# Gated attention with squares on ScalarE and inverse roots by tile, and a causal output projection of rounded parts

## The chip, the cores and the metric

The kernel runs on one core of a Trainium2 chip, as one launch. The metric is the device time in microseconds (us). A core has TensorE (PE, products; PEld is its loading of weights), VectorE (DVE), ScalarE (ACT), GpSimd (POOL) and SyncE (SP, which here issues every DMA). They run their own streams of instructions and meet at semaphores.

## The reference, cut to what matters

x has 16 tiles of 128 tokens with 256 features. Six layers are added to it in turn. Two are touched:

```
# layer 0: causal attention, 16 heads of 64
q, k, v = (layernorm(x) @ w_q, @ w_k, @ w_v)          # 256 -> 1024 each
out = softmax(causal(q k^T / 64)) v                   # per head
x = x + out @ w_u + b_u                               # 1024 -> 256

# layer 3: gated attention, 16 heads of 16
Q, K, V = (xn @ Wq.T + bq, ...)                       # 256 -> 256 each
Qn, Kn = Q / max(|Q|, 1e-12), K / max(|K|, 1e-12)     # per head
heads = softmax(Qn Kn^T / 4) V
heads = heads * sigmoid(g) * sigmoid(mean_tokens(gelu(xn @ Wg1.T + bg1) @ Wg2.T + bg2))
x = x + heads @ Wo.T + bo
```

All tensors are float32.

## The kernel before

Every layer is a stage with tensors and semaphores of its own, and a barrier between stages. A stage handles x in eight pairs of tiles (`PAIRS`); a pair i has tiles b = 0 and 1. Each engine's program is written out by hand inside a loop over the pairs (`pairs_by_two`: three turns of two pairs in a hardware loop, then two written out); work for later pairs stands between that for pair i. Nothing reorders it: what an engine does next is the order of its lines. `Chain.link` makes an engine wait for its own last instruction.

"Rounded parts": a float32 operand is split into a high part in TensorE's rounded format (fp32r) and a low part (what is left), and `split_product` makes one product out of three (high x high, high x low, low x high).

The causal stage (`stage_causal_attention`, `CausalAttention`; tensors a_...). `produce` makes slots of a ring of two banks with rounded parts of xn and of the weights (`w`, from `w_nat`, whose low parts VectorE makes in `weight_low`, one for each of q, k, v). A pair has eight units u of four heads: `pe_scores`, `dve_max`, `act_exp`, `dve_normalise` (probabilities times the inverse of their sum), `pe_transpose`, `copy_probT`, `pe_weighted`. Every second unit VectorE copies a chunk of 512 columns out of `out_bank` into `attnT` (`copy_out`, chunks 0 to 3; chunk 3 after the last unit). Then `pe_project` multiplies attnT with w_u, 8 products for each tile, in float32 without splitting, and `dve_residual` adds the result to x. GpSimd adds the bias b_u to x (`add_bias`) and takes the root for the layernorm (`ln.root`).

The gated stage (`stage_gated_attention`; also a_...). A ring of two banks turns through these slots; those named for a later pair are made that far ahead: xn (of i+2, transposed), hidden (i+1, the gate's), qk0 and qk1 (i+2, queries and keys of tile 0 and 1, 512 columns), logits (i+1), turn_q and turn_k (i+1, transposes of the scaled queries and keys), values (i+1). A slot waits until the slot two before it has been emptied. Beside them stand `scores(i, b)`, `weigh(i, b)` (probabilities times values, and times ones for the sums, into `out[b]`) and `project(i, b)`, into the same bank. VectorE: `empty` of qk adds the bias; `sum_squares` squares queries and keys of both tiles, sums per head and bounds the sum; GpSimd's `invert` raises the 64 sums to -1/2; `scale_heads` multiplies both tiles with it; `normalise` takes the reciprocal of the probabilities' sums and multiplies; `add_residual` adds to x. ScalarE empties xn, hidden (gelu), logits and turn_q and does the `exponentials`.

## Time and profile before

| | |
|---|---|
| runs, median of 3 | 2009.88 us (2009.46 to 2011.67) |
| profiled execution, its own time | 2011.48 us |
| its span in the profile | 2009.8 us |
| TensorE busy | 1842.6 us, 92% |
| VectorE busy | 1327.1 us, 66% |
| ScalarE busy | 649.5 us, 32% |
| GpSimd busy | 175.8 us, 9% |
| TensorE's granted clock, mean | 0.964 |

The span is what the profiled execution shows from its first to its last instruction; its own time has 1.7 us around it. Busy shares are over the whole span. In the profile's rows a tile keeps the name of its stage's prefix (a_ for both attention stages here; the causal one lies before 375 us, the gated one between 1143 and 1346 us). An instruction that waited shows in brackets how long its engine had been idle and who released it. [...]

### The profile page before, as it was taken

To read this page: it belongs to the slowest core of one execution; us is meant where nothing else is said; L and a number is where in the kernel's file an instruction comes from. 1 tells how busy PE (TensorE), PEld (TensorE's weight loads), DVE (VectorE), ACT (ScalarE), POOL (GpSimd) and SP (SyncE) were. 2 spreads that over 40 slices of the span, in tenths; PEclk is the share of its full clock that TensorE was granted. 3 is DMA by queue.
4 is the path that set the end of the run, shared out by engine and by line. 5 is a ranking of instruction groups with operands and counts; after the bars stand their busy time and mean duration, and the time that the engine had idled before them with its cause. 6 is when DMAs were issued, how large, how long until landed. Compare 5 with 4: busy or idle time off the path is not lost. (4 is left out here: it accounts for less than half of the span.)

```text
span 2009.8 us, 43767 instructions
## 1 busy us (share of the span) xinstructions
PE 1842.6 (92%) x16819; PEld 1541.4 (77%) x16819; DVE 1327.1 (66%) x3598; ACT 649.5 (32%) x1504; POOL 175.8 (9%) x125
## 2 busy tenths in 40 slices
PE   6999999699749999999999878878899999999998
PEld 5887787477638888888888645557788888888887
DVE  4555555377668988888988446646666666666664
ACT  3444434244342211221122035426333333323332
POOL 0000000011000000000000046531000000000000
PEclk9999999799879999999999879979899999999999
DMA  4000000222060000000000130001212010111101
GB/s 159 1 1 0 0 0 1 48 64 63 1 131 8 8 7 3 7 7 8 3 7 1 35 85 1 0 1 38 33 16 32 16 31 16 29 18 27 20 0 43
DMA packets 139319, 48.61 MB, mean 24 GB/s; under 512 B 108178, under 2 KB 138418, under 8 KB 139186
## 3 DMA queue, kind: packets, MB, share of 16 engines
q1 hardware_dynamic: 139186, 46.66, 10.4%
q8 instruction: 105, 1.72, 0.4%
q14 instruction: 28, 0.23, 0.0%
HBM read 42.43 MB, written 4.19 MB: 23 GB/s over the span
## 5 line engine op out<-in xcount | busy, mean ns | idle before, releaser
L2849 DVE TENSOR_TENSOR m_act_up<-m_silu,m_up 128x512 f32<-128x512 f32 x136 | 93.5, 687 | 168.0 <-PE m_up L587 125.0
L2768 ACT ACTIVATE m_silu<-m_gate 128x512 f32<-128x512 f32 x136 | 81.5, 599 | 379.6 <-PE m_gate L587 379.6
L2833 DVE SCALAR_TENSOR_TENSOR g_x<-m_y,m_combine,g_x 128x256 f32<-128x256 f32 x272 | 118.8, 479 | 52.8 <-PE m_y L587 51.3
L233 ACT ACTIVATE a_prob<-a_score,a_neg_max 128x128 f32<-128x128 f32 x256 | 90.7, 367 | 170.3 <-DVE a_neg_max L223 170.3
L2404 PE MATMUL f_out<-f_ko,f_gel 128*128 128x256 f32 x512 | 123.9, 394 | 2.4 <-issue 1.3
L2447 ACT ACTIVATE f_gel<-f_act 128x512 f32<-128x512 f32 x128 | 76.6, 598 | 131.7 <-PE f_act L587 90.9
L2404 PE MATMUL f_turn<-f_ko,f_gel 128*128 128x256 f32 x512 | 111.8, 379 | 0.0
L2404 PEld LDWEIGHTS f_out<-f_ko,f_gel 128*128 128x128 f32 x512 | 96.1, 194 | 17.1 <-issue 4.1
L587 PE MATMUL f_act<-f_hT_pair_high,f_kiT_high 128*128 128x256 f32 x384 | 108.2, 282 | 0.0
L2404 PEld LDWEIGHTS f_turn<-f_ko,f_gel 128*128 128x128 f32 x512 | 97.3, 190 | 13.2
L587 PE MATMUL f_act<-f_hT_pair_high,f_kiT_low 128*128 128x256 f32 x384 | 107.3, 279 | 0.0
L587 PE MATMUL f_act<-f_hT_pair_low,f_kiT_high 128*128 128x256 f32 x384 | 107.3, 279 | 0.0
L2839 DVE TENSOR_TENSOR m_hidden_low<-m_act_up,m_hidden_high 128x512 fp32r<-128x512 f32 x136 | 93.2, 685 | 1.5
L1281 POOL TENSOR_TENSOR a_inv<-a_ss,a_inv_power 128x64 f32<-128x64 f32 x8 | 84.6, 10571 | 71.7 <-DVE a_ss L1485 71.7
L2762 ACT CAST m_hidden_high<-m_act_up 128x512 fp32r<-128x512 f32 x136 | 83.4, 613 | 18.9 <-DVE m_act_up L2849 18.9
L587 PE MATMUL m_y<-g_wT_high,m_hidden_high 128*128 128x256 f32 x288 | 81.9, 284 | 2.9 <-DVE g_x L2833 1.9
L587 PE MATMUL m_y<-g_wT_high,m_hidden_low 128*128 128x256 f32 x288 | 81.8, 284 | 0.0
L587 PE MATMUL m_y<-g_wT_low,m_hidden_high 128*128 128x256 f32 x288 | 81.5, 283 | 0.0
L587 PE MATMUL a_ring<-a_xnT_high,a_w_high 128*128 128x256 f32 x256 | 77.1, 301 | 4.5 <-DVE a_w_low L544 4.4
L2437 ACT ACTIVATE g_shared<-g_shared 128x64 f32<-128x64 f32 x16 | 4.1, 256 | 235.8 <-DVE g_shared L2483 235.7
L587 PE MATMUL m_y<-m_wT_high,m_hidden_high 128*128 128x256 f32 x256 | 73.0, 285 | 1.9 <-DVE g_x L2833 1.9
L587 PEld LDWEIGHTS f_act<-f_hT_pair_high,f_kiT_high 128*128 128x128 f32 x384 | 72.0, 188 | 2.8 <-ACT f_gel L2447 1.4
(381 smaller groups left out, 5010.0 us busy)
## 6 DMA issues: line engine op xcount, KB each, us to landing
f_gel<-in_L_ffn_key_in SPq DMA_DIRECT2D x16, 256.0 KB, 4.9
f_ko<-in_L_ffn_key_out SPq DMA_DIRECT2D x2, 2048.0 KB, 18.5
g_shared<-in_ctx SPq DMA_DIRECT2D x8, 256.0 KB, 2.8
fp_wq_nat<-in_L_ffn_w_q SPq DMA_DIRECT2D x8, 256.0 KB, 3.1
h_kept<-fp_hT SPq DMA_DIRECT2D x8, 256.0 KB, 2.9
g_shared<-h_kept SPq DMA_DIRECT2D x8, 256.0 KB, 3.4
g_ctx_next<-in_ctx SPq DMA_DIRECT2D x8, 256.0 KB, 2.7
g_ctx_all<-in_ctx SPq DMA_DIRECT2D x1, 2048.0 KB, 10.3
```

The lines of the kernel that those rows point to most:

```text
L233: last = act.activation(self.prob[:, u % 4, j, :], self.score_bank[u % 2][:, j // 2, (j % 2) * P:(j % 2 + 1) * P], ACT.Exp, bias=self.neg_ ...
L587: ins = pe.matmul(dst, left[a], right[b], start=first and n == 0, stop=last and n == 2)
L1281: pool.tensor_tensor(inv[par][:, :], ss[par][:, :], inv_power[:, :], ALU.pow).then_inc(inverse_ready, 1)
L2404: last = pe.matmul(out_of(t), gel[:, r, t * P:(t + 1) * P], ko[:, r, :], start=(r == 0), stop=(r == R - 1))
L2437: act.activation(weight[:, :, :], weight[:, :, :], ACT.Exp).then_inc(weight_exp, 1)
L2447: act.activation(gel[:, rows_of(u):rows_of(u) + 2, :].rearrange("p r t -> p (r t)"), act_bank[q][:, :], ACT.Gelu).then_inc(act_used[q].sem, 1)
L2762: act.copy(hidden[0][:, g % 2, m, :], act_up[:, m, :]).then_inc(high_ready[m].sem, 1)
L2768: act.activation(silu[:, m, :], gate_bank[m][:, :], ACT.Silu).then_inc(silu_ready[m].sem, 1)
L2833: last = dve.scalar_tensor_tensor(x[:, tile, :], y_bank[n][:, t * D:(t + 1) * D], weight, x[:, tile, :], ALU.mult, ALU.add)
L2839: dve.tensor_tensor(hidden[1][:, g % 2, m, :], act_up[:, m, :], hidden[0][:, g % 2, m, :], ALU.subtract).then_inc(low_ready[m].sem, 1)
L2849: dve.tensor_tensor(act_up[:, m, :], silu[:, m, :], up_bank[m][:, :], ALU.mult) \
```

## The change

Causal stage: w_u and attnT are split into rounded parts. GpSimd makes both, by multiplying with one (high part) and subtracting (low part): w_u's at the start, attnT's after each chunk's copy. `pe_project` uses `split_product`, and waits for the parts of each half of a tile. w_u is loaded into the first third of `w_nat`, attnT lies in its second, so SP waits until the low part of w_q has been made before it issues w_u, b_u and the rest of x.

Gated stage: squares are made by ScalarE (`square`), sums, inverse roots and scaling are done per tile, the reciprocal of the sums is a step of its own (`invert_sums`), and the orders on all engines change.

```diff
+    def pool_parts(self, pool, i, c, high, low):
+        if c == 0:
+            self.part_links.begin(i)
+        pool.wait_ge(self.out_ready.sem, self.out_ready.at(i, c + 1))
+        if c == 0:
+            pool.wait_ge(self.projected, i)
+        self.part_links.link(pool, pool.tensor_tensor(high, self.attnT(c), self.one[:, 0:1].broadcast_to([P, 4 * P]), ALU.mult))
+        pool.tensor_tensor(low, self.attnT(c), high, ALU.subtract).then_inc(self.parts_ready.sem, 1)
...
+            half = len(pairs) // 2
             for n, (a, w) in enumerate(pairs):
-                last = pe.matmul(self.out_bank[:, b * D:(b + 1) * D], a, w, start=(n == 0), stop=(n == len(pairs) - 1))
+                if n % half == 0:
+                    pe.wait_ge(self.parts_ready.sem, self.parts_ready.at(i, 2 * b + n // half + 1))
+                last = split_product(pe, self.out_bank[:, b * D:(b + 1) * D], a, w, n == 0, n == len(pairs) - 1)
...
-        wu = s.sb("wu", [P, MT, D])
+        wu_nat = w_nat[:, 0, :, :].rearrange("p k (t d) -> p (k t) d", d=D)
+        wu = [s.sb(f"wu_{part}", [P, MT, D], F32R) for part in ("high", "low")]
...
-        attnT = s.sb("attnT", [P, 2, MT, P])
+        attnT = w_nat[:, 1, :, :].rearrange("p k (t q) -> p k t q", q=P)
+        attn_parts = [s.sb(f"attnT_{part}", [P, 2, MT, P], F32R) for part in ("high", "low")]
...
-            sp.dma_start(wu[:, :, :], w_u.rearrange("(k p) n -> p k n", p=P)).then_inc(out_loaded, 16)
+            sp.wait_ge(low_ready, 1)
+            sp.dma_start(wu_nat[:, :, :], w_u.rearrange("(k p) n -> p k n", p=P)).then_inc(out_loaded, 16)
...
+            pool.memset(att.one[:, :], 1.0).then_inc(att.one_set, 1)
+            pool.wait_ge(att.one_set, 1)
+            pool.tensor_tensor(wu[0][:, :, :], wu_nat[:, :, :],
+                               att.one[:, 0:1].unsqueeze(2).broadcast_to([P, MT, D]), ALU.mult).then_inc(wu_ready, 1)
+            pool.wait_ge(wu_ready, 1)
+            pool.tensor_tensor(wu[1][:, :, :], wu_nat[:, :, :], wu[0][:, :, :], ALU.subtract).then_inc(wu_ready, 1)
             for i, _ in pairs_by_two(pool):
                 att.add_bias(pool, i, x, bu, ln)
+                att.pool_parts(pool, i, 0, *[chunk_of(part, 0) for part in attn_parts])
                 ln.root(pool, i + 2)
+                for c in range(1, 4):
+                    att.pool_parts(pool, i, c, *[chunk_of(part, c) for part in attn_parts])
...
-            pe.wait_ge(out_loaded, 32)
+            pe.wait_ge(wu_ready, 2)
...
-            def invert(n, par):
-                pool.wait_ge(squares_ready, n + 1)
-                pool.tensor_tensor(inv[par][:, :], ss[par][:, :], inv_power[:, :], ALU.pow).then_inc(inverse_ready, 1)
+            def invert(n, par, b):
+                pool.wait_ge(squares_ready, 2 * n + b + 1)
+                pool.tensor_tensor(heads_of(inv[par], b), heads_of(ss[par], b), heads_of(inv_power, b), ALU.pow) \
+                    .then_inc(inverse_ready, 1)
...
-            invert(0, 0)
             ln.root(pool, 2)
-            invert(1, 1)
+            for n in range(2):
+                for b in range(2):
+                    invert(n, n, b)
             pool.wait_ge(loaded, N_LOADS * 16)
             for i, par in pairs_by_two(pool):
+                ln.root(pool, i + 3)
                 add_bias(i)
-                ln.root(pool, i + 3)
                 if exists(i + 2):
-                    invert(i + 2, par)
+                    for b in range(2):
+                        invert(i + 2, par, b)
...
                 produce(i, "qk0", par)
                 produce(i, "logits", 1 - par)
+                weigh(i, 1, par)
                 produce(i, "qk1", par)
                 produce(i, "turn_q", 1 - par)
+                project(i, 0)
                 produce(i, "turn_k", 1 - par)
-                project(i, 0)
-                weigh(i, 1, par)
+                project(i, 1)
                 if exists(i + 1):
                     ring.wait_emptied(pe, i, "turn_q")
                     ring.wait_emptied(pe, i, "turn_k")
                     scores(i + 1, 0)
                 produce(i, "values", 1 - par)
-                project(i, 1)
...
+            def square(i, n, par, b):
+                if not exists(n):
+                    return
+                ring.wait_emptied(act, i, f"qk{b}")
+                if not (isinstance(n, int) and n == 0):
+                    act.wait_ge(squares_ready, 2 * n - 1 + b)
+                act.activation(sq[:, b, :], qk[par][:, b, :], ACT.Square).then_inc(squared, 1)
...
+                empty(i, "hidden", i + 1, 1 - par)
                 empty(i, "xn", i + 2, par)
-                empty(i, "hidden", i + 1, 1 - par)
                 exponentials(i, 1)
                 empty(i, "logits", i + 1, 1 - par)
+                square(i, i + 2, par, 0)
                 empty(i, "turn_q", i + 1, 1 - par)
+                square(i, i + 2, par, 1)
...
-            def sum_squares(i, n, par):
+            def sum_squares(n, par, b):
                 if not exists(n):
                     return
-                square_links.begin(n)
-                ring.wait_emptied(dve, i, "qk1")
-                square_links.link(dve, dve.tensor_tensor(sq[:, :, :], qk[par][:, :, :], qk[par][:, :, :], ALU.mult))
-                square_links.link(dve, dve.tensor_reduce(ss[par][:, :], sq[:, :, :].rearrange("p b (h d) -> p (b h) d", d=HD),
-                                                  AX.X, ALU.add))
-                dve.tensor_scalar(ss[par][:, :], ss[par][:, :], NORM_EPS2, None, ALU.max).then_inc(squares_ready, 1)
-
-            def scale_heads(n, par):
+                if b == 0:
+                    square_links.begin(n)
+                sums = heads_of(ss[par], b)
+                dve.wait_ge(squared, 2 * n + b + 1)
+                square_links.link(dve, dve.tensor_reduce(sums, sq[:, b, :].rearrange("p (h d) -> p h d", d=HD), AX.X, ALU.add))
+                dve.tensor_scalar(sums, sums, NORM_EPS2, None, ALU.max).then_inc(squares_ready, 1)
+            def scale_heads(n, par, b):
                 if not exists(n):
                     return
-                dve.wait_ge(inverse_ready, n + 1)
-                heads = qk[par][:, :, :].rearrange("p b (h d) -> p (b h) d", d=HD)
-                dve.tensor_tensor(heads, heads, inv[par][:, :].unsqueeze(2).broadcast_to([P, 4 * NH, HD]), ALU.mult) \
-                    .then_inc(scaled, 1)
+                dve.wait_ge(inverse_ready, 2 * n + b + 1)
+                heads = qk[par][:, b, :].rearrange("p (h d) -> p h d", d=HD)
+                dve.tensor_tensor(heads, heads, heads_of(inv[par], b).unsqueeze(2).broadcast_to([P, 2 * NH, HD]),
+                                  ALU.mult).then_inc(scaled, 1)
...
+            def invert_sums(i, b):
+                dve.wait_ge(weighted.sem, weighted.at(i, b + 1))
+                dve.reciprocal(inv_sum[:, b, :, :].rearrange("p t q -> p (t q)"), out[b][:, D:2 * D]).then_inc(sum_inverted.sem, 1)
             def normalise(i, b, par):
-                dve.wait_ge(weighted.sem, weighted.at(i, b + 1))
+                dve.wait_ge(sum_inverted.sem, sum_inverted.at(i, b + 1))
                 dve.wait_ge(gate_ready, i + 1)
-                if b == 0:
-                    norm_links.begin(i)
-                norm_links.link(dve, dve.reciprocal(inv_sum[:, b, :, :].rearrange("p t q -> p (t q)"), out[b][:, D:2 * D]))
...
+            ln.apply(dve, 1)
             empty(-2, "qk1", 0, 0)
-            sum_squares(-2, 0, 0)
-            ln.apply(dve, 1)
             ln.statistics(dve, 2)
+            sum_squares(0, 0, 0)
+            sum_squares(0, 0, 1)
             empty(-1, "qk0", 1, 1)
+            ln.apply(dve, 2)
             empty(-1, "qk1", 1, 1)
-            sum_squares(-1, 1, 1)
-            ln.apply(dve, 2)
-            scale_heads(0, 0)
+            sum_squares(1, 1, 0)
+            sum_squares(1, 1, 1)
+            scale_heads(0, 0, 0)
+            scale_heads(0, 0, 1)
             finish_gate(-1, 0, 0)
             empty(-1, "turn_k", 0, 0)
             dve.wait_ge(v_zeroed, 2)
             empty(-1, "values", 0, 0)
             for i, par in pairs_by_two(dve):
                 ln.statistics(dve, i + 3)
+                scale_heads(i + 1, 1 - par, 0)
+                invert_sums(i, 0)
                 empty(i, "qk0", i + 2, par)
                 normalise(i, 0, par)
-                scale_heads(i + 1, 1 - par)
+                scale_heads(i + 1, 1 - par, 1)
+                sum_squares(i + 2, par, 0)
+                invert_sums(i, 1)
                 empty(i, "qk1", i + 2, par)
+                normalise(i, 1, par)
                 empty(i, "turn_k", i + 1, 1 - par)
                 add_residual(i, 0)
-                sum_squares(i, i + 2, par)
-                normalise(i, 1, par)
+                add_residual(i, 1)
+                sum_squares(i + 2, par, 1)
                 finish_gate(i, i + 1, 1 - par)
+                ln.apply(dve, i + 3)
                 empty(i, "values", i + 1, 1 - par)
-                ln.apply(dve, i + 3)
-                add_residual(i, 1)
```

TensorE, inside the gated loop, from the logits of one pair on. a_hsum is the gate's hidden sum, a_xnT with a_wT of 128x512 a query-key product, a_qk what is turned, a_attnT what is projected. Before:

```order
L1321 MATMUL a_ring<-a_hsum,a_wg_wide 128x2 x2
L765 REGISTER_ALU
L729 MATMUL a_ring<-a_wT,a_xnT 128x512 x2
L765 REGISTER_ALU
L1330 REGISTER_ALU
L1334 MATMUL a_ring<-g_ident,a_qk 128x128 x4
L765 REGISTER_ALU
L1334 MATMUL a_ring<-g_ident,a_qk 128x128 x4
L1365 ISA
L1367 MATMUL a_out<-a_wT,a_attnT 128x256 x2
L1359 MATMUL a_out<-a_probT,a_v 32x128 x16
L1359 MATMUL a_out<-a_probT,a_ones 32x128 x16
```

and from the weighing of tile 1 of one pair of the change:

```order
L1363 MATMUL a_ring<-a_hsum,a_wg_wide 128x2 x2
L1401 MATMUL a_out<-a_probT,a_v 32x128 x16
L1401 MATMUL a_out<-a_probT,a_ones 32x128 x16
L799 REGISTER_ALU
L763 MATMUL a_ring<-a_wT,a_xnT 128x512 x2
L799 REGISTER_ALU
L1372 ISA
L1376 MATMUL a_ring<-g_ident,a_qk 128x128 x4
L1407 ISA
L1409 MATMUL a_out<-a_wT,a_attnT 128x256 x2
L799 REGISTER_ALU
L1376 MATMUL a_ring<-g_ident,a_qk 128x128 x4
```

The weighing of tile 1 (a_v and a_ones) has moved from behind the first projection to ahead of the second query-key product, and a projection stands between turned queries and turned keys.

VectorE, inside the gated loop, from the reciprocal of tile 0. Before:

```order
L1511 RECIPROCAL a_inv_sum<-a_out 128x256
L62 REGISTER_ALU
L1513 SCALAR_TENSOR_TENSOR a_attnT<-a_out,a_gate,a_inv_sum 128x128 x2
L1490 REGISTER_ALU
L1492 TENSOR_TENSOR a_qk<-a_qk,a_inv 128x1024
L773 REGISTER_ALU
L1470 TENSOR_TENSOR a_qk<-a_ring,a_bqk 128x512
L773 REGISTER_ALU
L1474 COPY a_kT<-a_ring 128x512
L1521 ISA
L1521 TENSOR_TENSOR g_x<-a_out,g_x 128x256
```

and of the change, from the same reciprocal:

```order
L1565 RECIPROCAL a_inv_sum<-a_out 128x256
L807 ISA
L1527 TENSOR_TENSOR a_qk<-a_ring,a_bqk 128x512
L1571 SCALAR_TENSOR_TENSOR a_attnT<-a_out,a_gate,a_inv_sum 128x128 x2
L1547 REGISTER_ALU
L1549 TENSOR_TENSOR a_qk<-a_qk,a_inv 128x512
L1540 ISA
L1541 TENSOR_REDUCE a_ss<-a_sq 128x32
L1542 TENSOR_SCALAR a_ss<-a_ss 128x32
L1564 REGISTER_ALU
L1565 RECIPROCAL a_inv_sum<-a_out 128x256
```

The scaling (a_qk from a_qk and a_inv) has come apart into two of 512 columns, the squares (a_sq) are gone from here, and the reciprocal (a_inv_sum) of tile 1 stands ahead of the second bias instead of behind the residual.

GpSimd, start of the causal stage up to the loop's first instructions. Before:

```order
L149 TENSOR_TENSOR a_ln_rstd<-a_ln_var_eps,a_ln_power 128x2 x2
L635 UNCONDITIONAL_BRANCH
L635 ISA
L298 ISA
L298 TENSOR_TENSOR g_x<-g_x,a_bu 128x512
L148 REGISTER_ALU
L149 TENSOR_TENSOR a_ln_rstd<-a_ln_var_eps,a_ln_power 128x2
```

and of the change:

```order
L149 TENSOR_TENSOR a_ln_rstd<-a_ln_var_eps,a_ln_power 128x2 x2
L437 MEMSET a_one 128x1
L439 TENSOR_TENSOR a_wu_high<-a_w_nat,a_one 128x2048
L442 TENSOR_TENSOR a_wu_low<-a_w_nat,a_wu_high 128x2048
L669 UNCONDITIONAL_BRANCH
L669 ISA
L302 ISA
L302 TENSOR_TENSOR g_x<-g_x,a_bu 128x512
L309 ISA
L312 TENSOR_TENSOR a_attnT_high<-a_w_nat,a_one 128x512
L62 ISA
L313 TENSOR_TENSOR a_attnT_low<-a_w_nat,a_attnT_high 128x512
```

Two passes over w_u stand ahead of the loop, and each chunk of attnT (now inside a_w_nat) brings two passes of 512 columns.

## Rows read from the trace of the kernel before

**Rows 1.** Busy time per engine in stretches: causal loop, gated loop.
```profile
42.00:373.00 331.00, 321.76 (x2508) 258.78 (x2506) 181.76 (x369) 135.35 (x584) 13.03 (x13) 0.99 0.00 1
1190.10:1291.30 101.20, 84.88 (x1025) 58.14 (x1021) 68.11 (x143) 49.32 (x77) 56.64 (x16) 1.00 0.00 1
```

**Rows 2.** Timeline of TensorE, one gated pair: start, us, what [idle <-releaser].
```profile
1210.82 0.66 PE L166 MATMUL a_ring<-g_ident,a_ln_xn 128*128 128x128 f32 x4 [0.60 <-DVE a_ln_xn L156]
...
1218.01 1.98 PE L729 MATMUL a_ring<-a_wT,a_xnT 128*128 128x512 f32 x4 [0.44 <-DVE a_qk L1470]
1221.54 1.17 PE L1334 MATMUL a_ring<-g_ident,a_qk 128*128 128x128 f32 x8 [1.55 <-DVE a_qk L1492]
...
1229.20 1.13 PE L1367 MATMUL a_out<-a_wT,a_attnT 128*128 128x256 f32 x4 [0.73 <-DVE a_attnT L1513]
1230.93 0.66 PE L166 MATMUL a_ring<-g_ident,a_ln_xn 128*128 128x128 f32 x4 [0.60 <-DVE a_ln_xn L156]
```

**Rows 3.** Timeline of VectorE, gated stage.
```profile
1205.21 1.22 DVE L1483 TENSOR_REDUCE a_ss<-a_sq 128x64 f32<-128x1024 f32 x1
...
1210.04 0.72 DVE L156 TENSOR_SCALAR a_ln_xn<-g_x,a_ln_mv,a_ln_rstd 128x256 f32 x2
...
1217.88 1.75 DVE L1511 RECIPROCAL a_inv_sum<-a_out 128x256 f32<-128x256 f32 x1
1219.66 0.61 DVE L1513 SCALAR_TENSOR_TENSOR a_attnT<-a_out,a_gate,a_inv_sum 128x128 f32<-128x128 f32 x2
1220.18 1.22 DVE L1492 TENSOR_TENSOR a_qk<-a_qk,a_inv 128x1024 f32<-128x1024 f32 x1
```

**Rows 4.** Timeline of TensorE, ahead of and behind the gated loop.
```profile
1182.19 1.94 PE L1334 MATMUL a_ring<-g_ident,a_qk 128*128 128x128 f32 x8 [5.40 <-DVE a_qk L1492]
...
1320.31 1.94 PE L1334 MATMUL a_ring<-g_ident,a_qk 128*128 128x128 f32 x8 [4.92 <-DVE a_qk L1492]
...
1336.36 1.95 PE L1367 MATMUL a_out<-a_wT,a_attnT 128*128 128x256 f32 x4 [2.53 <-DVE a_attnT L1513]
```

**Rows 5.** Timeline of TensorE, causal stage.
```profile
41.83 0.39 PE L211 MATMUL a_score<-g_causal_bf,g_ident_bf 128*128 128x256 bf16 x2 [1.44 <-ACT a_prob L233]
...
79.33 7.17 PE L307 MATMUL a_out_bank<-a_wu,a_attnT 128*128 128x256 f32 x32 [0.16 <-DVE a_attnT L273]
...
88.15 0.28 PE L587 MATMUL a_ring<-a_xnT_high,a_w_high 128*128 128x256 f32 x1
...
90.54 0.28 PE L587 MATMUL a_ring<-a_xnT_high,a_w_low 128*128 128x256 f32 x1
```

**Rows 6.** Timeline of GpSimd, causal stage.
```profile
20.41 1.27 POOL L298 TENSOR_TENSOR g_x<-g_x,a_bu 128x512 f32 x1 [7.09 <-DMA a_bu<-in_L_attn_b_u]
```

**Rows 7.** Timeline of VectorE and of GpSimd, gated stage, two passes at once.
```profile
1317.89 2.27 DVE L1492 TENSOR_TENSOR a_qk<-a_qk,a_inv 128x1024 f32<-128x1024 f32 x1 [0.57 <-POOL a_inv L1281]
...
1317.82 3.47 POOL L1286 TENSOR_TENSOR g_x<-g_x,a_bo 128x512 f32<-128x512 f32 x2
```

**Rows 8.** Timeline of VectorE, start of the causal stage.
```profile
14.44 2.29 DVE L544 TENSOR_TENSOR a_w_low<-a_w_nat,a_w_high 128x2048 fp32r<-128x2048 f32 x1
...
23.09 2.28 DVE L544 TENSOR_TENSOR a_w_low<-a_w_nat,a_w_high 128x2048 fp32r<-128x2048 f32 x1
...
29.21 2.28 DVE L544 TENSOR_TENSOR a_w_low<-a_w_nat,a_w_high 128x2048 fp32r<-128x2048 f32 x1
```

**Rows 9.** DMA issues up to 60 us: size each, us to landing.
```profile
a_w_nat<-in_L_attn_w_q SPq DMA_DIRECT2D x1, 1024.0 KB, 5.9
...
g_x<-in_x SPq DMA_DIRECT2D x1, 512.0 KB, 3.9
```

**Rows 10.** Timeline of ScalarE, gated stage.
```profile
1215.53 1.94 ACT L1440 ACTIVATE a_probT<-a_score 128x1024 f32<-128x1024 f32 x2
```

**Rows 11.** Timeline of GpSimd, gated stage, and operations on one tile.
```profile
1206.74 10.55 POOL L1281 TENSOR_TENSOR a_inv<-a_ss,a_inv_power 128x64 f32<-128x64 f32 x1 [13.87 <-DVE a_ss L1485]
...
L2076 POOL TENSOR_TENSOR fp_token_rstd<-fp_token_eps,fp_power x1: 2910/2910/2910, 545.9 to 545.9; 128x16 f32<-128x16 f32 x1
```

More of the change, by code:

```diff
@@ L196, in __init__ @@
         self.out_ready = s.counting("out_ready", self.chunks + 1)
+        self.part_links = Chain(s.sem("part_links"), self.chunks)
+        self.parts_ready = s.counting("parts_ready", self.chunks)
+        self.one = s.sb("one", [P, 1])
+        self.one_set = s.sem("one_set")
         self.projected = s.sem("projected")
@@ L388, in stage_causal_attention @@
         low_ready = s.sem("low_ready")
+        wu_ready = s.sem("wu_ready")
         xn_high = s.counting("xn_high", 1)
@@ L475, in _ @@
                 produce(i + 2, 1)
-                att.pe_project(pe, i, lambda b: [(attnT[:, b, t, :], wu[:, t, :]) for t in range(MT)])
+                att.pe_project(pe, i, lambda b: [([part[:, b, t, :] for part in attn_parts], [part[:, t, :] for part in wu])
+                                                 for t in range(MT)])
         def empty(eng, n, r, par, scaled_copy):
@@ L1264, in _, with heads_of @@
             load_next(sp)
+        def heads_of(sums, b):
+            return sums[:, 2 * NH * b:2 * NH * (b + 1)]
         @block.gpsimd
@@ L1329, in produce @@
                 else:
-                    pe.wait_ge(scaled, n + 1)
+                    pe.wait_ge(scaled, 2 * n + 2)
                     at = 0 if name == "turn_q" else D
@@ L1446, in _ @@
             act.activation(static[:, :], g_row[:, :], ACT.Exp, scale=-1.0).then_inc(static_exp, 1)
+            square(-2, 0, 0, 0)
             empty(-1, "xn", 1, 1)
+            square(-2, 0, 0, 1)
             empty(-1, "hidden", 0, 0)
+            square(-1, 1, 1, 0)
             act.wait_ge(wide_ready, 1)
             empty(-1, "logits", 0, 0)
+            square(-1, 1, 1, 1)
             empty(-1, "turn_q", 0, 0)
```

8 lines of the change are left out of this document (5 added, 3 removed).

## Prediction

> **What bounds the kernel now.** I read the busy times of stretches first [rows 1]: in the causal stage's loop TensorE is busy 321.76 of 331.00 us, so there its own instructions are the time, and a wait elsewhere is free unless it reaches TensorE. In the gated stage's loop it is busy 84.88 of 101.20 us (five pairs): a sixth is waiting. Then the order of time on TensorE through one steady gated pair [rows 2]: from transposes at 1210.82 to transposes at 1230.93 are 20.11 us, and four waits stand in it, 0.44 us (the second query-key product, for VectorE to empty the bank), 1.55 (the turned queries, for the scaled heads), 0.73 (the second projection, for the weighed tile), 0.60 (the transposes, for xn). Everything else there is back to back. Behind the 1.55 stands a chain on VectorE [rows 3]: reciprocal 1.75, two products 0.61, scaling of 1024 values 1.22, all after the query-key bias, while TensorE has only one product left. The pair before last waits 4.92 us and the last waits 2.53 us (and once more as long) [rows 4].
>
> **The causal projection.** Now it is 32 rows in 7.17 us per pair [rows 5], fp32 at half pace. It becomes 48 rounded products of the same shape as the ring's, which start every (90.54 - 88.15)/20 = 0.12 us [rows 5]: 47 x 0.12 + 0.28 = 5.9 us. TensorE is the bound, so 1.27 us x 8 pairs = 10.2 us are gained, if GpSimd's parts are there. It adds two passes of 128x512 for each of four chunks; one pass took 1.27 us [rows 6]. Chunk 3 is copied just before the projection; its parts are ready some 2.9 us later (two passes, two handovers of about 0.15), and TensorE first has 36 products = 4.3 us to do: 1.4 us of cover. If it went, the projection would wait by what is missing. GpSimd gets 8 x 1.27 = 10.2 us more per pair of some 41 (331.00/8): idle room.
>
> What GpSimd's passes do to VectorE I read from a collision [rows 7]: VectorE's scaling (two inputs in SBUF) starts at 1317.89, 0.07 us after GpSimd's bias pass, and takes 2.27 instead of 1.22 us, and the two bias passes take 3.47 instead of 2.54: one waited for the other, in turn. In the loop VectorE's probability scaling meets a parts pass about twice per pair and is late by 0.6 us, but its block is turned only a unit later (about 5 us): nothing, with 0 to 1.3 us per pair as bounds (one whole pass).
>
> **The start.** w_u now loads into w_nat's first third, so SP issues it only when the first low part is done, 14.44 + 2.29 = 16.7 us [rows 8]. 512 KB of x took 3.9 us to land and a first weight of twice that took 5.9 behind it [rows 9]; I take 4.7 for w_u and 0.5 more for b_u: 22.0, and GpSimd's two 128x2048 passes begin at 22.5 (21.7 to 23.6). At four times 1.27 us each takes 5.1. VectorE wants the second low part at 23.09 and the third at 29.21 [rows 8], both with two SBUF inputs. I take GpSimd to be first: the second low part then starts at 27.6, 4.5 us late, and TensorE's keys wait for it. GpSimd's second pass follows it from 29.9 to 35.0, the third low part, now wanted at 33.7, waits 1.3. That is 5.8 us. A TensorE that idled this long runs slower afterwards: after its 4.92 us idle, the eight turning transposes took 1.94 instead of 1.17 us [rows 2, 4]. So +6 us, bounds 0 (no collision) and 8. TensorE's own new wait, for both parts of w_u (35 us), stands ahead of 41.83 [rows 5] and is free. x's other tiles queue behind w_u and land near 27, before VectorE asks for them (about 39).
>
> **The gated loop.** Removed on VectorE: the squares, priced by the reduction's 1.22 us for 1024 values [rows 3]. Squares go to ScalarE, two of 128x512, 0.5 to 0.6 us each (half of one of the two 128x1024 exponentials, 1.94 together [rows 10], and a fixed part); it was busy 49.32 of 101.20 us [rows 1], so 1.2 per pair fits. The built program has no further table load for them. Scaling and reduction are split: 2 x 0.7 for 1.22, and 2 x 0.85 for 1.42. GpSimd's inverse of 64 columns took 10.55 us and one of 16 columns 2.91 [rows 11]: 0.159 per column plus 0.37, so 32 columns cost 5.5, two of them 10.9.
>
> Now one pair in the new order, from the end of the previous values product (0). TensorE's steps are those of [rows 2]: transposes to logits take 7.19 less the 0.44 waited, 6.75 us; the second query-key product 1.98 with its tail; turning, projection, weighing, scores and values 7.66 less 0.73, 6.93; the other projection 1.13 with its tail; 16.5 without the tails (about 0.15 each). VectorE's are those of [rows 3]. Transposes 0 to 0.5; hidden waits for VectorE to empty values (four of 128x128), 1.1 to 2.1: a new wait of 0.6. Scores to 3.2, weighing of tile 0 to 5.1, first query-key product to 6.9, logits to 7.4, weighing of tile 1 to 9.3 (its exponentials end near 6.9, as now), second query-key product to 11.1, turned queries to 11.6, projection 0 to 12.6, turned keys to 13.1, projection 1 to 14.1, scores to 15.2, values to 17.0. VectorE beside it: statistics to 2.3; half a scaling (its inverse is from the pair before) to 2.9; reciprocal of tile 0 from 5.3 to 7.0; bias 7.7; products 8.2; second half scaling 8.8; reduction 9.7; reciprocal of tile 1 to 11.5; bias 12.1 (turned keys want it at 12.6); products 12.7 (projection 1 wants them at 13.1); keys' copy 13.3 to 14.0 (scores want it at 14.1); residuals 14.7, reduction 15.5, gate, xn 16.5, values. So all four waits are gone, with 0.1 to 0.5 us to spare, and one of 0.6 is new. GpSimd: first inverse 9.8 to 15.3, second 15.5 to 21.0, root and bias by 6 of the next pair, needed at 8.2 and later: covered. The period is 17.1, 3.0 less, for six pairs (0 to 5): 18.1 us.
>
> Pair 6: its wait of 4.92 went to an inverse that started late; both inverses are now ready at 4 of this pair. With projection 1's 0.73 and less the new 0.6: 4.8. Pair 7: projection 0 now waits for reciprocal 0 (1.75) and two products (0.61) with nothing of TensorE's between, 2.53 us, and projection 1 the same again. In the new order weighing 1 (1.9 us) stands ahead of projection 0 and hides most of the first wait, and reciprocal 1 runs while projection 0 does; what is left is about 0.6 and 1.3, but weighing 1 has left the path too: 5.1 gained (3.2 of waits, 1.9 of the weighing), bounds 3 and 6. Ahead of the loop TensorE waited 5.40 us for the first scaling until 1182.19 [rows 4]. That scaling no longer stands behind an inverse of 10.55 that starts only when both tiles' squares are summed: the first half starts a product earlier, and VectorE has two passes of 1.22 fewer. I take half of the wait, 2.5; bounds 0 and 5.4. Sum 18.1 + 4.8 + 5.1 + 2.5 = 30.5.
>
> [...] Two scalings of xn took 0.72 us at 1210.04 [rows 3] in the middle of an inverse (10.55 us, begun at 1206.7): they were not held up. [...]
>
> **Sum**, against the profiled execution's own time of 2011.48 (span 2009.8, 1.7 around it), the run's median 2009.88 being 1.6 less: -10.2 + 6 - 30.5 = -34.7. On the median: **1975**.
>
> **Rivals.**
> - VectorE comes first at the start, or the passes don't collide: 0 to 1.3 lost instead of 6; about 1970. For it: 0.6 us decide, and the landing is an estimate. 0.16.
> - The gated period comes to 18.5, not 17.1: VectorE's chain through the reciprocals has 0.1 to 0.5 us of slack, and one late link repeats. 6 x 1.4 = 8 more: 1983. Against it, VectorE was busy 68.11 of 101.20 us [rows 1] and gets less to do. 0.14.
> - Parts passes reach TensorE in the causal loop, by one pass per pair, 1.3 x 8 = 10: the projection gains nothing: 1985. 0.05.
> - [...] 0.01. [...]
> - Slower: an inverse of 32 columns costs as much as one of 64. GpSimd then needs 2 x 10.55 + 1.27 + 0.7 = 23.1 us per pair and becomes the bound: 3 more for each of seven pairs instead of less, 10 more ahead of the loop: -10.2 + 6 + 21 + 10 - 5 = +22, 2032. It decides from about 9 us per inverse. Against it: 16 and 64 columns lie on one line [rows 11]. 0.03.
> - It doesn't do what it says: some wait keeps the pair at 20 and the start eats the projection's gain: 2006 to 2012. 0.01.
>
> **Numbers.** Likeliest (0.60) 1975. The range 1964 to 1988 takes in the bounds of the start (0 to 8), half a us per pair either way, and the first three rivals. Faster by over 0.2% (4 us, about what a measurement of this kernel can tell) 0.95, within it 0.02, slower 0.03.
>
> **What will show it.** Projection rows of 48 in 5.9 us with no wait for GpSimd; w_low's second instance 6 to 7 us long or late, and TensorE's first pair starting near 47 instead of 41.8; gated transposes 17.1 us apart; inverses of 5.5 us; no wait before the turned queries. Wrong would make it: a slower rounded product at this place, a table load per square, inverses over 7 us.

## Result and the profile after

The changed kernel took 1972.26 us (median of 4 runs, 1969.71 to 1975.05) against 2009.89 us of the kernel before beside it (2009.46 to 2011.67): a ratio of 0.9814 with a 95% interval of 0.9802 to 0.9826. The profiled execution's span was 1973.3 us, 36.5 us less than before. Three stretches of its trace in the view of busy times, with the columns of [rows 1] (the last three are granted clock, DMA share and GB/s), of which the first is the causal stage's loop, as in [rows 1], and the second the gated stage's first five pairs:

```profile
42.00:373.00 331.00, 315.07 (x2666) 257.99 (x2665) 196.09 (x382) 137.95 (x594) 93.32 (x79) 0.99 0.00 1
1181.60:1266.60 85.00, 82.26 (x1024) 59.82 (x1021) 63.16 (x151) 54.28 (x87) 63.01 (x21) 1.00 0.00 1
540.00:550.00 10.00, 10.00 (x49) 9.64 (x48) 5.17 (x30) 3.22 (x6) 2.91 (x1) 0.50 0.01 2
```

TensorE was busy 315.07 of the causal loop's 331.00 us and 82.26 of 85.00 us in the gated loop, where the same five pairs took 101.20 us [rows 1]. The third stretch lies in the product-key stage, which the change leaves alone; it is spoken of below. TensorE's timeline through one steady gated pair answers to [rows 2]:

```profile
1249.73 0.60 PE L166 MATMUL a_ring<-g_ident,a_ln_xn 128*128 128x128 f32 x4
1250.87 1.13 PE L1358 MATMUL a_ring<-a_xnT,a_wT 128*128 128x256 f32 x4 [0.54 <-DVE a_v L756]
...
1254.91 1.98 PE L763 MATMUL a_ring<-a_wT,a_xnT 128*128 128x512 f32 x4
...
1257.16 1.08 PE L1401 MATMUL a_out<-a_probT,a_v 128*32 128x128 f32 x32
...
1259.04 1.99 PE L763 MATMUL a_ring<-a_wT,a_xnT 128*128 128x512 f32 x4
1260.86 0.60 PE L1376 MATMUL a_ring<-g_ident,a_qk 128*128 128x128 f32 x4
1261.30 1.03 PE L1409 MATMUL a_out<-a_wT,a_attnT 128*128 128x256 f32 x4
1262.17 0.60 PE L1376 MATMUL a_ring<-g_ident,a_qk 128*128 128x128 f32 x4
1262.60 1.03 PE L1409 MATMUL a_out<-a_wT,a_attnT 128*128 128x256 f32 x4
...
1266.64 0.60 PE L166 MATMUL a_ring<-g_ident,a_ln_xn 128*128 128x128 f32 x4
```

From transposes to transposes are 16.91 us instead of 20.11. Of the four waits none is left, and the new one at hidden, 0.54 us, waits for VectorE to write the values. The second weighing (1257.16) now stands between the two query-key products (1254.91 and 1259.04). The timeline of VectorE for the same pair:

```profile
1255.04 1.76 DVE L1565 RECIPROCAL a_inv_sum<-a_out 128x256 f32<-128x256 f32 x1 [2.44 <-PE a_out L1401]
...
1259.46 1.76 DVE L1565 RECIPROCAL a_inv_sum<-a_out 128x256 f32<-128x256 f32 x1
...
1265.25 0.73 DVE L156 TENSOR_SCALAR a_ln_xn<-g_x,a_ln_mv,a_ln_rstd 128x256 f32 x2
...
1268.78 0.68 DVE L1549 TENSOR_TENSOR a_qk<-a_qk,a_inv 128x512 f32<-128x512 f32 x1
```

The timeline of GpSimd, its two inverses in one row:

```profile
1259.63 10.91 POOL L1320 TENSOR_TENSOR a_inv<-a_ss,a_inv_power 128x32 f32<-128x32 f32 x2 [4.11 <-DVE a_ss L1542]
```

Each tile's reciprocal of 1.76 us follows its weighing; the two inverses take 10.91 us together; each tile's scaling takes 0.69, a pair later (1268.78 is the next pair's first). The second inverse of the pair by itself:

```profile
1265.11 5.43 POOL L1320 TENSOR_TENSOR a_inv<-a_ss,a_inv_power 128x32 f32<-128x32 f32 x1
```

The scaling of xn (two in 0.73 us) began 0.14 us into it, the scaling of the heads at 1268.78 ran in its middle, and neither was held up.

At the start of the causal stage a cost was forecast. The timeline of TensorE there:

```profile
36.03 0.50 PE L621 MATMUL a_ring<-a_w_high,a_xnT_high 128*128 128x512 f32 x1 [4.24 <-DVE a_w_low L578]
...
37.03 0.63 PE L621 MATMUL a_ring<-a_w_high,a_xnT_high 128*128 128x512 f32 x1
...
47.86 0.39 PE L215 MATMUL a_score<-g_causal_bf,g_ident_bf 128*128 128x256 bf16 x2 [1.44 <-ACT a_prob L237]
```

The timeline of VectorE, its second and third low part of the input weights:

```profile
23.44 2.28 DVE L578 TENSOR_TENSOR a_w_low<-a_w_nat,a_w_high 128x2048 fp32r<-128x2048 f32 x1
...
29.55 6.42 DVE L578 TENSOR_TENSOR a_w_low<-a_w_nat,a_w_high 128x2048 fp32r<-128x2048 f32 x1
```

The timeline of GpSimd, the two passes over w_u and the first bias pass:

```profile
24.91 4.27 POOL L439 TENSOR_TENSOR a_wu_high<-a_w_nat,a_one 128x2048 fp32r<-128x2048 f32 x1
29.26 4.57 POOL L442 TENSOR_TENSOR a_wu_low<-a_w_nat,a_wu_high 128x2048 fp32r<-128x2048 f32 x1
33.78 3.33 POOL L302 TENSOR_TENSOR g_x<-g_x,a_bu 128x512 f32 x1
```

VectorE's low part at 23.44 took its 2.28 us, and GpSimd's first pass, begun at 24.91 beside it, 4.27 (3.60 in e3_late_split below, where no low part ran beside it). The low part at 29.55 met the second pass, begun 0.29 us before it, and took 6.42: it was done 2.1 us after that pass, so nearly all its work came behind it. TensorE waited 4.24 us for it. From 36.61 its 128x512 products started 0.43 us apart until 40.0, at a mean granted clock of 0.50, and 0.23 apart after that, at 1.00 (40 to 42 us). The first pair starts at 47.86, 6.03 us later than before [rows 5].

Where the 36.5 us lie, from the two traces: the causal stage's last projection row is at 367.7 instead of 371.8, 4.1 less; from there to the first transposes of the gated stage, code that the change leaves alone, 778.7 instead of 776.0, 2.7 more; from there to the next stage's first row 164.8 instead of 201.4, 36.6 less; behind that 1.5 more.

### The profile page after: what moved, and what is told of

Read it like the earlier page. It is cut to its first block and busy times, and to the rows that moved or that the text cites. A ratio compares the mean times of both kernels' runs of the same rounds, so it can differ in the third digit from the quotient of the medians.

```text
span 1973.3 us, 44245 instructions
## 1 busy us (share of the span) xinstructions
PE 1824.4 (92%) x16947; PEld 1539.4 (78%) x16947; DVE 1331.3 (67%) x3614; ACT 658.1 (33%) x1520; POOL 268.0 (14%) x200
## 3 DMA queue, kind: packets, MB, share of 16 engines
q1 hardware_dynamic: 139186, 46.66, 10.3%
## 5 line engine op out<-in xcount | busy, mean ns | idle before, releaser
L1320 POOL TENSOR_TENSOR a_inv<-a_ss,a_inv_power 128x32 f32<-128x32 f32 x16 | 86.9, 5438 | 26.2 <-DVE a_ss L1542 26.0
```

Of the source, the lines that this page charges most:

```text
L1320: pool.tensor_tensor(heads_of(inv[par], b), heads_of(ss[par], b), heads_of(inv_power, b), ALU.pow) \
```

## Experiments

**The two halves apart.** Two kernels, each with one half of the diff.

The first, e1_causal_only, is the changed kernel with stage_gated_attention as it was before, all hunks of it; its loop on TensorE shows it:

```diff
-                weigh(i, 1, par)
                 produce(i, "qk1", par)
                 produce(i, "turn_q", 1 - par)
-                project(i, 0)
                 produce(i, "turn_k", 1 - par)
-                project(i, 1)
+                project(i, 0)
+                weigh(i, 1, par)
...
                 produce(i, "values", 1 - par)
+                project(i, 1)
```

> The causal stage of the changed kernel with the gated stage of the kernel before. Theory (the start gives back what the projections gain): the causal stage ends 4.1 us earlier than before, as in the changed kernel (last projection row at 367.70 instead of 371.84), and what follows is the kernel before up to a change in when TensorE's clock falls, so 2006 us (2003 to 2009). Rival (the start costs nothing in the end and the projections give the 10.2 us of the prediction): 2000 us. In the trace: first pair near 47.9, pairs 41.8 apart.

Measured: 2006.52 us (11 runs, ratio 0.9983, 0.9974 to 0.9992). The last causal row is at 368.3, the first pair starts at 48.3 and the later pairs are 41.8 apart; in the changed kernel these are 367.7, 47.9 and 41.8. The theory holds: the half is worth 2.9 us (1.6 to 5.2), because the start takes back a good part of what the projections give.

The second, e2_gated_only, is the changed kernel with all of CausalAttention and stage_causal_attention as before:

```diff
-                att.pe_project(pe, i, lambda b: [([part[:, b, t, :] for part in attn_parts], [part[:, t, :] for part in wu])
-                                                 for t in range(MT)])
+                att.pe_project(pe, i, lambda b: [(attnT[:, b, t, :], wu[:, t, :]) for t in range(MT)])
```

> The causal stage of the kernel before with the gated stage of the changed one. Theory (the two halves add up): the gated stage is 35.6 us shorter by the traces, so 2009.9 - 35.6 = 1974 us (1972 to 1978), with 16.9 us between pairs in the loop. Rival (the gain ahead of the loop in the changed kernel, 7.1 us where 2.5 were forecast, came only from how the clock stood when the stage was reached): the stage starts with the clock of the kernel before and gains 4.6 us less, 1979 us.

Measured: 1980.86 us (4 runs, ratio 0.9856, 0.9840 to 0.9873), pairs 16.91 us apart. The gated stage takes 168.8 us, 32.7 less than before, and not the 36.6 of the changed kernel's trace: the rival holds. Between the two traces, 3.8 us are the part ahead of the loop (35.2 us in the changed kernel's, 39.0 here), where the mean granted clock was 0.76 there and is 0.60 here. The first query-key product of the stage in TensorE's timeline, first of the changed kernel, then of this run:

```profile
1154.44 1.98 PE L763 MATMUL a_ring<-a_wT,a_xnT 128*128 128x512 f32 x4 [0.26 <-ACT a_wg2T L725]
```

```profile
1156.18 3.78 PE L729 MATMUL a_ring<-a_wT,a_xnT 128*128 128x512 f32 x4 [0.26 <-ACT a_wg2T L691]
```

It is the same work behind the same wait: 1.98 us at a granted clock of 1.00 (1154.44 to 1156.42), 3.78 us at 0.50 (1156.18 to 1159.90). Nor is 35.2 what the change always gives: in the eight other traces whose code ahead of the loop is the changed kernel's, word for word, the part took 35.2 to 37.8 us. The halves' medians add up to 31.5 us less (27 to 37 by their intervals), the whole change gives 37.6 (35 to 40): the intervals overlap only from 35 to 37. The spans of the single traces do add up (5.6 and 30.8 for the halves, 36.5 for the whole). So whether the halves give less than the whole stays open; of the 6 us between the medians the clock ahead of the loop can be up to 3.8.

**The collision at the start.**

```diff
+            pool.wait_ge(low_ready, 3)
             pool.memset(att.one[:, :], 1.0).then_inc(att.one_set, 1)
```

> The changed kernel; GpSimd starts the splitting of w_u only when VectorE's third low part of the input weights is written. Theory (the third low part, 6.42 us instead of 2.28, is held up by GpSimd's second pass over w_u, and TensorE's wait of 4.24 us at 36.03 is nothing else): w_low's third instruction takes 2.3 us, the wait at 36 is gone, the first pair starts near 42.5 instead of 47.9 and the time is 4 to 6 us less, 1967 us. Rival (the passes then run at 32 to 41 us and hold up VectorE's emptying of the first products or the first layer norm): the first pair starts no earlier than 46 and the time is within 2 us of 1972.

Measured: 1968.06 us (5 runs, ratio 0.9786, 0.9773 to 0.9800). The timeline of TensorE at the first pair's scores, and then that of VectorE at the third low part:

```profile
42.11 0.39 PE L215 MATMUL a_score<-g_causal_bf,g_ident_bf 128*128 128x256 bf16 x2 [1.44 <-ACT a_prob L237]
```

```profile
29.52 2.28 DVE L579 TENSOR_TENSOR a_w_low<-a_w_nat,a_w_high 128x2048 fp32r<-128x2048 f32 x1
```

The low part takes 2.28 us, the wait is gone, and the first pair starts at 42.11, 5.75 earlier: 4.2 of the wait and 1.6 of eight products at a granted clock of 0.50 (0.43 instead of 0.23 us each; here the clock was 1.00). In the medians 3 to 4 us of it are left (1968.06 against 1972.26 and, in e11_changed_again, 1970.84), by the ratios 5 to 6; the intervals of the ratios just touch. The theory holds; GpSimd's passes, now from 32.1 to 40.3, hold up nothing that TensorE waits for.

**The one wait left in the gated pair.**

```diff
-                produce(i, "hidden", 1 - par)
                 scores(i, 1)
+                produce(i, "hidden", 1 - par)
                 ring.wait_emptied(pe, i, "values", -1)
...
+                empty(i, "xn", i + 2, par)
                 empty(i, "hidden", i + 1, 1 - par)
-                empty(i, "xn", i + 2, par)
                 exponentials(i, 1)
```

> The changed kernel; in the gated loop TensorE multiplies the scores of the second tile ahead of the hidden layer, and ScalarE empties xn ahead of hidden. Theory (the one wait of a steady pair, 0.54 us at hidden for VectorE's writing of the values, is bare and nothing else is due): it is covered by the scores, pairs are 16.37 us apart instead of 16.91, 6 of them and the like at the ends 3 to 4 us less: 1969 us. Rival (the exponentials of the second tile, then behind a later hidden on ScalarE, come late for the weighing): the wait moves there and the time is within 1 us of 1972, or some 3 us above.

Measured: 1971.82 us (6 runs, ratio 0.9794, 0.9771 to 0.9817). Pairs are 16.38 us apart, exactly as the theory has it, but the first takes 17.91 instead of 17.41, and the time of six runs went from 1958.72 at a mean granted clock of 0.973 to 1978.09 at 0.962. The mechanism is shown; that the time fell is not.

**The second tile's weighing put back behind the first projection.**

```diff
-                weigh(i, 1, par)
                 produce(i, "qk1", par)
                 produce(i, "turn_q", 1 - par)
                 project(i, 0)
+                weigh(i, 1, par)
                 produce(i, "turn_k", 1 - par)
```

> The changed kernel with one order of TensorE taken back: in the gated loop the second tile is weighed behind the first tile's projection instead of ahead of the second query-key product. Theory (this place is what opens VectorE's chain early: reciprocal of the sums 1.76 us, emptying of qk1 0.63, normalising 0.68 stand behind the weighing on it): the weighing ends at about 13 us of the pair instead of 9.8, turn_k's bank comes 2.4 us late, pairs are 19.3 us apart instead of 16.9, and the time is 17 us more, 1989 us. Rival (the place doesn't matter once the inverses go by tile): pairs stay under 17.3 and the time under 1976.

Measured: 2005.77 us (10 runs, ratio 0.9978, 0.9963 to 0.9993), 33 us more than the changed kernel, twice the forecast. Rows of TensorE's timeline in its steady pair:

```profile
1225.26 1.98 PE L763 MATMUL a_ring<-a_wT,a_xnT 128*128 128x512 f32 x4 [0.44 <-DVE a_qk L1527]
...
1229.37 1.06 PE L1401 MATMUL a_out<-a_probT,a_ones 128*32 128x128 f32 x32
1232.86 0.66 PE L1376 MATMUL a_ring<-g_ident,a_qk 128*128 128x128 f32 x4 [2.42 <-DVE a_qk L1527]
```

Pairs are 20.07 us apart, 0.04 less than in the kernel before (two of the five in the loop take 21.4). The turned keys' wait of 2.42 us is the one forecast. Left out of the forecast were 0.44 at the second query-key product, there again as before the change, and the last two pairs: from the last transposes to the next stage are 58.5 us instead of 44.6. With this one order taken back, the rest of the gated half gives almost nothing.

**Squares back on VectorE.**

```diff
-                dve.wait_ge(squared, 2 * n + b + 1)
+                ring.wait_emptied(dve, n - 2, f"qk{b}")
+                square_links.link(dve, dve.tensor_tensor(sq[:, b, :], qk[par][:, b, :], qk[par][:, b, :], ALU.mult))
```

> The changed kernel with the squares taken back from ScalarE to VectorE (two of 0.69 us for each pair, just ahead of each sum). Theory (VectorE is not the bound of the pair, 13.7 of 16.9 us busy, but the first of the two stands ahead of the second reciprocal, behind which turn_k's bank is freed): 0.5 us more for each pair, 17.4 us apart, and the time 3 to 5 us more, 1976 us. Rival (everything on VectorE in the pair counts in full): 1.4 us for each pair, 18.3 us apart, 1982 us. Rival (covered altogether): 16.9 us and 1972.

Measured: 1976.04 us (4 runs, ratio 0.9828, 0.9797 to 0.9860), pairs 17.35 us apart. 0.44 us of the 1.4 reach the pair, as the theory has it; the time alone, 4 us more, is not clear of the changed kernel's. VectorE has room; where the work stands on it decides.

**One inverse for both tiles.**

```diff
-                pool.wait_ge(squares_ready, 2 * n + b + 1)
-                pool.tensor_tensor(heads_of(inv[par], b), heads_of(ss[par], b), heads_of(inv_power, b), ALU.pow) \
-                    .then_inc(inverse_ready, 1)
+                if b == 0:
+                    return
+                pool.wait_ge(squares_ready, 2 * n + 2)
+                pool.tensor_tensor(inv[par][:, :], ss[par][:, :], inv_power[:, :], ALU.pow).then_inc(inverse_ready, 2)
```

> The changed kernel with one inverse root of 64 columns for each pair (10.5 us) instead of two of 32 (5.44 us each), started at the second tile's sum. Theory (it is the first inverse, begun 5.5 us ahead of the second sum, that lets the next pair's first scaling start on time; now the scaling waits 6.8 us and everything on VectorE stands behind it): a loop of sum, inverse 10.5 and VectorE's 11 to 13 us from the scaling to the next sum, so 22 to 24 us between pairs and 35 to 50 us more, 2015 us, slower than the kernel before. Rival (the inverse is hidden as it was before the change, the gain is the order's and the squares'): pairs under 17.5 us, time under 1978.

Measured: 2000.88 us (7 runs, ratio 0.9954, 0.9938 to 0.9970). VectorE's longest wait over four pairs:

```profile
engine line waited for: us in total, times, longest us
DVE a_qk L1550 <- POOL a_inv L1322: 27.8, 4, 7.0
```

The timeline of GpSimd, two inverses in a row:

```profile
1217.12 10.56 POOL L1322 TENSOR_TENSOR a_inv<-a_ss,a_inv_power 128x64 f32<-128x64 f32 x1 [8.91 <-DVE a_ss L1543]
...
1237.99 10.56 POOL L1322 TENSOR_TENSOR a_inv<-a_ss,a_inv_power 128x64 f32<-128x64 f32 x1 [8.42 <-DVE a_ss L1543]
```

Pairs are 20.8 to 20.9 us apart, and VectorE's scaling waits 7.0 us in each: the mechanism of the theory. Its period of 22 to 24 was too long: from the end of the inverse to the next are 20.87 - 10.56 = 10.3 us, less than the 11 to 13 that I took; VectorE, late itself, waits for TensorE only 1.1 us per pair (4.4 in four; at the first reciprocal alone it waits 2.44 in the changed kernel), which may be why. So it costs 29 us, not 35 to 50.

**Both edits that stood for themselves.** The diffs of e3_late_split and e4_scores_first together.

> The changed kernel with both edits that stood for themselves before: the splitting of w_u behind the third low part (median 1968.1, 4.2 us less) and the second tile's scores ahead of the hidden layer (pairs 16.38 us apart instead of 16.91, but 0.5 us more at the first pair and at the last). Theory (they add up, 4.2 and 0.53 x 5 less 1.0): 1966 us (1962 to 1969). Rival (the second edit gives nothing, since its median of 1971.8 was that of the changed kernel): 1968 us. In the trace: first pair at 42.5, pairs 16.38 us apart.

Measured: 1964.55 us (5 runs, ratio 0.9777, 0.9751 to 0.9802), the fastest of all. The order that covers the values' writing, in TensorE's timeline:

```profile
1208.21 0.60 PE L166 MATMUL a_ring<-g_ident,a_ln_xn 128*128 128x128 f32 x4
1208.74 1.16 PE L1390 MATMUL a_score<-a_qM,a_kT 32*128 32x256 f32 x16
1209.83 1.13 PE L1359 MATMUL a_ring<-a_xnT,a_wT 128*128 128x256 f32 x4
...
1224.60 0.60 PE L166 MATMUL a_ring<-g_ident,a_ln_xn 128*128 128x128 f32 x4
```

Hidden (1209.83) stands behind the scores, no row of the pair waits, and pairs are 16.38 to 16.39 us apart. Against e3_late_split alone (0.9786) the intervals overlap: only that it beats the kernel before, by 45 us, is certain; it is probably ahead of the changed one, mostly by the start.

**The cover of the parts.** GpSimd writes each high part twice in e9_double_high.

```diff
-        self.part_links.link(pool, pool.tensor_tensor(high, self.attnT(c), self.one[:, 0:1].broadcast_to([P, 4 * P]), ALU.mult))
+        for _ in range(2):
+            self.part_links.link(pool, pool.tensor_tensor(high, self.attnT(c), self.one[:, 0:1].broadcast_to([P, 4 * P]), ALU.mult))
```

In e10_four_high the 2 is a 4.

> The changed kernel; GpSimd writes each attention high part twice. Theory (the passes are covered: chunk 3's parts are then ready 1.1 us later, 3.6 us behind the first projection row, and TensorE wants them after 36 products, 4.3 us; what a pass costs is that VectorE's scaling of the probabilities beside it takes 0.95 us instead of 0.69): TensorE waits for no parts, pairs are 41.8 to 42.0 us apart, and the time is 0 to 2 us more than 1972. Rival (cover already used up at one pass, or each pass costs in full): 1.0 us and more for each pair, 1980 us.

Measured: 1971.01 us (4 runs, ratio 0.9823, 0.9804 to 0.9841), pairs 41.8 us apart: a pass of 1.04 us more per chunk costs nothing.

> The changed kernel; GpSimd writes each attention high part four times. Theory (the cover is 36 products, 4.3 us): chunk 2's passes now end 0.6 us behind chunk 3's copy, chunk 3's parts are ready 6.0 us behind the first row, TensorE waits 1.7 us in each projection, pairs are 43.6 us apart and the time is 12 to 16 us more, 1986 us. Rival (GpSimd is never waited for): 41.8 to 42.2 us apart, 1974 us.

Measured: 2001.04 us (4 runs, ratio 0.9955, 0.9938 to 0.9972), pairs 44.8 us apart. The view of waits, for TensorE in one of them:

```profile
engine line waited for: us in total, times, longest us
PE a_out_bank L622 <- POOL a_attnT_low L314: 2.2, 1, 2.2
PE a_probT_bank L253 <- DVE a_probT L260: 0.9, 2, 0.7
PE a_out_bank L622 <- DVE a_w_nat L277: 0.2, 1, 0.2
```

TensorE waits 2.2 us for the last parts, after 36 rows that take 4.4 us: the edge is where I had put it. But the pair grows by 3.0 us, forecast were 1.7: 0.6 more go to the turning of the probabilities (waits of 0.9 against 0.3 in a pair of the changed kernel), where VectorE's scaling took up to 1.26 us instead of 0.69. Three pairs took 46.3, and in the last projection TensorE waited for parts twice, 3.2 and 4.0 us. So the time is 30 us more and not the 12 to 16 of the theory, whose cover was right and whose price was not.

**The changed kernel again.**

> The changed kernel itself once more, to have more of its times beside those of the kernel before on one chip. Theory (the times of one kernel differ by how much of the span TensorE's clock is granted): a median of 1972 us, single spans between 1962 and 1980, each lower the higher its mean granted clock, at the same 41.8 and 16.9 us between pairs. Rival (the median of 1972.3 of four runs was by chance): a median off by more than 3 us.

Measured: 1970.84 us (5 runs, ratio 0.9811, 0.9798 to 0.9824). Its pairs are 41.8 and 16.91 us apart as before, and yet its span of 1968.5 is 4.8 less than the first trace's. One place where the two part, the third stretch shown above, here of this run:

```profile
540.00:550.00 10.00, 9.23 (x80) 8.90 (x79) 5.59 (x27) 6.15 (x13) 2.91 (x1) 0.96 0.01 2
```

The granted clock was 0.96 here and 0.50 in the other execution, in the same code. By the gated stage's start, 4.5 us lie between the two traces; ahead of the gated loop this one takes 37.0 us at a mean granted clock of 0.68, 1.8 more than the first. That each time is lower the higher its mean clock, as the theory says, did not show in these five runs, which lie within 2.8 us: the fastest, 1968.52, had the lowest, 0.967. In the six of e4_scores_first it did.

## Why the prediction was right

**The time.** 1975 was forecast, 1972.3 and 1970.8 were measured; the reading of what bounds each stage held. Inside the causal stage two sizes were off by 1.5 us each, in opposite directions.

**The projections.** Forecast: 1.27 us x 8 = 10.2. From the first row of the projection to the next unit's row are now 5.85 us; before, 7.01 and not 7.17, whose last 0.16 is the modelled end of a row that overlaps the next. And the first row comes 0.08 us later. So a steady pair gains 1.08 (42.89 to 41.81 us), and the eight projections 8.7 us, not 10.2. From the first pair to the last row the stage did gain 10.2, but 1.5 of it lie ahead of the first projection row, where the change takes no work from TensorE. The busy times from the first pair to that row, first before, then after:

```profile
41.83:79.33 37.50, 37.03 (x301) 29.75 (x301) 23.08 (x48) 19.08 (x83) 1.96 (x2) 0.95 0.00 1
```

```profile
47.86:83.87 36.01, 35.47 (x301) 28.21 (x301) 24.62 (x49) 18.97 (x83) 8.40 (x8) 1.00 0.01 1
```

The same 301 instructions of TensorE took 1.5 us less at a granted clock of 1.00 instead of 0.95: in the kernel before, the ring's 128x256 products from 43.97 to 46.10 start 0.21 us apart (clock 0.50) and not 0.12 (1.00).

**Parts behind VectorE's work.** The scaling of the probabilities took 0.692 us before the change, and now on the average (the view of groups, busy us and mean ns, of VectorE in four pairs):

```profile
L246 DVE TENSOR_TENSOR a_prob<-a_prob,a_norm 128x512 f32<-128x512 f32 x32 | 24.2, 756 | 1.1
```

The forecast held: one waits for the other, two per pair are held up by 0.26, and nothing of it reaches TensorE beyond the 0.08; doubling the passes (e9_double_high) changed nothing.

**The start.** Forecast +6, measured +6.03 at the first pair, and this is the place where the size was right for a wrong reason. w_u landed 5.6 us after its issue and b_u 7.2, not 4.7 and 0.5 more (w_u has 1024 KB, as many as the first weight, whose 5.9 stood in [rows 9]), so the splitting began at 24.9, not 22.5. VectorE was first at the second low part, which lost nothing instead of 4.5, and GpSimd 0.29 us ahead of it at the third, which lost 4.1 instead of 1.3. GpSimd was ahead at the third in all nine traces with this start, by 0.08 to 0.31 us. In seven of them its first pass met the second low part and took 3.88 to 4.31 us instead of 3.60, as if held until VectorE was done; a landing up to 0.7 us later would then have changed nothing (an estimate from these rows: the second low part ended at 25.72).

Nor are the 6.03 us the whole account. The stretch at a granted clock of 0.50 that the forecast counts as new, behind the wait, was in the kernel before as well, in its first pair (43.97 to 46.10); after the change it lies ahead of it (36.61 to 40.0). At the first projection row the changed kernel is 4.5 us behind (83.87 against 79.33), about the wait of 4.24. So the start cost 1.5 less than forecast and the projections gave 1.5 less: -4.2 were forecast for the stage and -4.1 measured, and that they agree so closely is luck.

**The gated pair.** Forecast 17.1, measured 16.91, with the one wait of 0.6 (0.54) where it was put. The tight places stand as forecast: giving VectorE 0.69 us more ahead of the second reciprocal costs 0.44 per pair (e6_vector_squares). Ahead of the loop 2.5 were forecast: 3.3 in e2_gated_only, 5.3 and 7.1 in the changed kernel's two traces, at granted clocks of 0.60, 0.68 and 0.76. From the sixth pair on 13.3 were gained in e2_gated_only; the forecast has 12.9 for it (3.0, 4.8 and 5.1, where the 4.8 is a slip: its own terms, 4.92 + 0.73 - 0.6, give 5.05). So the stage is worth 32.7 in e2_gated_only and 34.8 and 36.6 in the changed kernel's traces, forecast 30.5.

**Sum.** Causal stage -4.1, gated stage by itself -32.7, together -36.8, forecast -34.7; the medians give -37.6 and -38.3.

**The rivals.** VectorE first at the start: it was, at one of the two. The inverse of 32 columns took 5.44 us, so GpSimd isn't the bound. VectorE was not held up through the inverses: xn was scaled in 0.73 us at 1265.25 and the heads in 0.68 at 1268.78, both inside one of 5.43 us. A slower period through a late link didn't come either, but e5_weigh_behind and e7_whole_inverse show how near it stood: the second weighing's place or the inverses by tile, taken back alone, lose 29 to 33 of its 33 us.

## What to carry to other kernels

When two engines feed each other in turn, each new order or finer grain may be worth nothing alone: the second weighing's place and the inverses by tile, each taken back alone, lost nearly the whole gain. Lay out the whole pair for both engines and look for the tight places before removing a wait. And where a GpSimd pass over two tensors in SBUF can meet a VectorE pass on which TensorE waits, keep them apart by a wait on the later one, if its result has time: here the VectorE pass took 6.42 us beside the GpSimd pass and 2.28 without it, and the wait gave 3 to 6 us for one line.

## What the runs showed of the hardware

The times of one kernel lay 3 to 19 us apart (e4_scores_first from 1958.72 to 1978.09, its mean granted clock from 0.973 to 0.962 with them), while the changed kernel's steady gated pairs agreed to 0.02 us in two traces. The traces part in the product-key stage (0.50 and 0.96 from 540 to 550 us, behind a wait of 2.96 us in both) and ahead of the gated loop, where TensorE idles for some us at a time (the longest waits were 7.34 and 7.23 us in the changed kernel's trace, 7.35 and 5.23 in its second): there the clock was 0.58, 0.67, 0.60, 0.76 and 0.68 in five traces (before, e1_causal_only, e2_gated_only, changed, changed again), and code that is the same in all took 773.3 to 778.7 us between the two changed stages. A stretch at a clock of 0.50 also moved: it lay in the first causal pair before the change (43.97 to 46.10), ahead of it after (36.61 to 40.0), and in e3_late_split and e8_late_and_first the clock was 1.00 throughout from 32 to 79 us. What decides when the clock falls these runs do not show. So stage spans of single traces differ by 2 to 5 us without any cause in the code, and gains of that size are to be read in steady periods.

An inverse root (power) on GpSimd let VectorE pass: two scalings of xn in 0.73 us, and the scaling of the heads, with two inputs in SBUF, in 0.68 us in the middle of it (1268.78; the inverse took 5.43 us from 1265.11). A subtraction of two tensors, of 1.63 us, did not. VectorE's timeline with GpSimd's beside it, in the causal loop:

```profile
114.77 1.71 DVE L156 TENSOR_SCALAR a_ln_xn<-g_x,a_ln_mv,a_ln_rstd 128x256 f32 x2
```

```profile
114.38 1.63 POOL L313 TENSOR_TENSOR a_attnT_low<-a_w_nat,a_attnT_high 128x512 fp32r<-128x512 f32 x1
```

The same two scalings of xn took 1.71 us here, the first of them 1.38 instead of 0.41: it ended 0.14 us behind the subtraction.
